# Attention blocks 8 to 14: who turns the probabilities, and when the next scores come

## What is computed

```python
def self_attn(x, Wq, Wk, Wv):
    Q, K, V = (x @ Wq, x @ Wk, x @ Wv)
    energy = jnp.einsum('bqd,bkd->bqk', Q, K)
    ...
    causal = (kidx[None, :] > kidx[:, None])[None]
    energy = jnp.where(pad | causal, NEG_INF, energy)
    score = jax.nn.softmax(energy / np.sqrt(DK), axis=-1)
    return jnp.einsum('bqk,bkd->bqd', score, V)
```

## Time and profile before

| | us |
|---|---|
| median of 3 runs | 1653.44 |
| lowest, highest | 1651.63, 1654.49 |
| profiled execution, whole | 1656.21 |
| its span, first to last instruction | 1654.4 |
| PE busy | 1617.4 |
| DVE busy | 862.5 |
| ACT busy | 572.2 |

### The profile page before, as it was taken

The page is one execution under the profiler, slowest core; times in us unless marked ns, Lnnn a source line. Parts: engine busy times, 40 slices in busy tenths (PEclk is TensorE's granted clock), DMA queues, the critical chain, the costliest instruction groups (busy, mean ns, idle before and its releaser), DMA issues. The chain is left out here.

```text
span 1654.4 us, 20692 instructions
## 1 busy us (share of the span) xinstructions
PE 1617.4 (98%) x7634; PEld 1334.5 (81%) x7634; DVE 862.5 (52%) x1760; ACT 572.2 (35%) x990; POOL 367.2 (22%) x562
## 2 busy tenths in 40 slices
PE   8999999999999999899999899999999999999999
PEld 6887888877788887678787687888888888888887
DVE  6757444477664435678888955342333232423311
ACT  5432121134221112466566533332323232323322
POOL 1212100022220100388888911000000000000000
PEclk9999999999999999799999999999999999999999
DMA  6302110131220104445545344121211112121100
GB/s 212 105 22 96 45 52 26 39 115 58 70 77 33 45 26 164 138 135 162 165 154 172 102 160 120 58 44 52 51 52 46 57 38 64 39 64 32 45 1 26
DMA packets 129930, 130.88 MB, mean 79 GB/s; under 512 B 70769, under 2 KB 70769, under 8 KB 129675
## 3 DMA queue, kind: packets, MB, share of 16 engines
q1 hardware_dynamic: 128032, 126.10, 24.5%
q10 hardware_dynamic: 1797, 3.46, 0.6%
HBM read 87.34 MB, written 42.18 MB: 78 GB/s over the span
## 5 line engine op out<-in xcount | busy, mean ns | idle before, releaser
L747 PE MATMUL banks<-split_q,split 128*128 128x512 f32 x2328 | 568.1, 393 | 4.6 <-POOL split L1563 3.2
L747 PE MATMUL banks<-split 128*128 128x512 f32 (+5 forms) x2304 | 543.1, 385 | 10.8 <-DVE split L1688 5.9
L747 PEld LDWEIGHTS banks<-split_q,split 128*128 128x128 f32 x2328 | 433.4, 188 | 96.9 <-POOL split L1563 4.1
L747 PEld LDWEIGHTS banks<-split 128*128 128x128 f32 (+3 forms) x2304 | 414.5, 185 | 107.0 <-issue 8.1
L747 PE MATMUL banks<-split,split_q 128*128 128x512 f32 (+3 forms) x1728 | 392.4, 379 | 6.8 <-DVE split_q L1688 4.1
L747 PEld LDWEIGHTS banks<-split,split_q 128*128 128x128 f32 x1728 | 308.7, 189 | 57.9 <-DVE split_q L1688 4.9
L2194 DVE TENSOR_TENSOR split<-plain,split 128x512 fp32r<-128x512 f32 x128 | 88.4, 691 | 385.6 <-ACT split L1464 385.6
L1458 ACT ACTIVATE plain<-banks,small 128x512 f32<-128x512 f32 x128 | 88.2, 689 | 400.1 <-PE banks L747 400.1
L1688 DVE TENSOR_TENSOR split<-banks,split 128x512 fp32r<-128x512 f32 (+5 forms) x232 | 146.3, 638 | 152.9 <-ACT split L1145 152.3
L1145 ACT ACTIVATE split<-banks 128x512 fp32r<-128x512 f32 (+5 forms) x232 | 124.4, 557 | 247.2 <-PE banks L957 191.1
L1497 POOL TENSOR_TENSOR small<-small 128x1 f32<-128x1 f32 x64 | 13.1, 205 | 475.7 <-DVE small L1724 475.5
(11 more groups left out here) (156 smaller groups left out, 1275.3 us busy)
## 6 DMA issues: line engine op xcount, KB each, us to landing
plain<-in_x SPq DMA_DIRECT2D x64, 256.0 KB, 2.7
xo_scratch<-plain SPq DMA_DIRECT2D x32, 256.0 KB, 2.3
x_scratch<-plain SPq DMA_DIRECT2D x32, 256.0 KB, 2.0
plain<-x_scratch SPq DMA_DIRECT2D x32, 256.0 KB, 3.0
tile_x<-xo_scratch SPq DMA_DIRECT2D x32, 256.0 KB, 3.1
xg_scratch<-tile_x SPq DMA_DIRECT2D x32, 256.0 KB, 2.1
out<-plain SPq DMA_DIRECT2D x32, 256.0 KB, 2.1
tile_x<-x_scratch SPq DMA_DIRECT2D x28, 256.0 KB, 4.6
```

The lines of the kernel that those rows point to most:

```text
L747: mm = nc.tensor.matmul(out, left(c, l), right(c, r), start=start and c == 0 and (l, r) == PASSES[0], stop=stop and c == chunks - 1 and (l ...
```

## The change

`turned(i)` marks blocks 8 to 14 of each batch. For these:

- PE issues no T. SP stores each chunk of the row buffer to `p_scratch` as soon as `p_ready` comes (`store_p`), and loads it back in four transfers for each chunk with the squares exchanged (`load_p`). All stores of a block come first, then all its loads. They stand at the end of SP's iteration i-2, behind the store of x1 for block i-2.
- A new letter I: DVE transposes within the squares, from the row buffer into the bank that T used. The high and low parts (still letter T, for ACT and DVE) follow as before.
- The list has another order: all of S(i+1) stands ahead of V(i) on PE. In blocks 8, 9, 10, 12, 13 and 14, I comes behind S(i+1, 1); V(i, 0) comes behind the last S, and on ACT the parts of chunk 2 stand behind X(i+1). In block 11 the projections Q(3, m) stand around the first parts, and V(11, 0) ahead of the scores.

```diff
+        if turned(i) and n1 > n0:
+            g = i // 4 + 1
+            order += [("Q", g, 0), end[0], ("Q", g, 1), end[1], ("I", i, 0), ("I", i, 1), ("Q", g, 2), ("T", i, 0),
+                      ("Q", g, 3), ("T", i, 1), ("V", i, 0), ("I", i, 2), ("S", i + 1, 0), ("T", i, 2)]
+            order += [("S", i + 1, c) for c in range(1, n1)]
+            order += [("X", i + 1, 0), ("V", i, 1), ("V", i, 2)]
+        elif turned(i):
+            order += [end[0], ("S", i + 1, 0), ("S", i + 1, 1), ("I", i, 0), ("I", i, 1), ("T", i, 0), ("I", i, 2),
+                      ("S", i + 1, 2), ("T", i, 1)]
+            order += [("I", i, 3)] if n0 > 3 else []
+            order.append(end[1])
+            order += [("S", i + 1, 3)] if n0 > 3 else []
+            order += [("X", i + 1, 0), ("V", i, 0), ("T", i, 2), ("V", i, 1)]
+            order += [("T", i, 3)] if n0 > 3 else []
+            order += [("V", i, c) for c in range(2, n0)]
...
-            if kind == "T":
+            if kind == ("I" if turned(i) else "T"):
                 order.append(("p", b, i, c))
...
+                def store_p(i, c):
+
+                    n, at, w = squares_in(b, i, c), c * 512, width_of(i, c)
+                    if n > 1:
+                        sp.wait_ge(p_in[c], (n - 1) * QB * 16)
+                    sp.dma_start(p_dram[c, 0:P * w].rearrange("(p n) -> p n", n=w), Srow[:, i % 2, at:at + w]).then_inc(p_out[c], 16)
+
+                def load_p(i, c):
+
+                    at, w = c * 512, width_of(i, c)
+                    sp.wait_ge(p_out[c], squares_in(b, i, c) * 16)
+                    squares_of = p_dram[c, 0:P * w].rearrange("(q s c i r) -> i s c q r", q=QB, s=32, i=QB, r=32)
+                    for n in range(QB):
+                        sp.dma_start(Srow[32 * n:32 * n + 32, i % 2, at:at + w].rearrange(
+                            "p (c q r) -> p c q r", q=QB, r=32), squares_of[n]).then_inc(p_in[c], 16)
...
+                    if turned(i + 2):
+                        sp.wait_ge(p_ready, b * NB + i + 2 + 1)
+                        for c in range(chunks_of(i + 2)):
+                            store_p(i + 2, c)
+                        for c in range(chunks_of(i + 2)):
+                            load_p(i + 2, c)
...
-                    elif kind == "T":
+                    elif kind == "T" and not turned(i):
                         n = TURNS["p", b, i, c]
                         if c == 0:
                             pe.wait_ge(p_ready, b * NB + i + 1)
+                        if c == 0 and turned(i - 1):
+                            pe.wait_ge(tp_full, n)
                         pe.wait_ge(tp_free, n + 1)
...
+                    elif kind == "I":
+                        n, at, w = TURNS["p", b, i, c], c * 512, width_of(i, c)
+                        dve.wait_ge(p_in[c], squares_in(b, i, c) * QB * 16)
+                        dve.wait_ge(tp_free, n + 1)
+                        nc.vector.transpose(PS[:, 2 + n % 2, 0:w], Srow[:, i % 2, at:at + w]).then_inc(tp_full, 1)
```

More of the change, by code:

```diff
@@ L89, with turned, squares_in @@
 T_BEFORE = [sum(chunks_of(j) for j in range(i)) for i in range(NB + 1)]
+def turned(i):
+    return 8 <= i < NB - 1
+def squares_in(b, i, c):
+    return sum(turned(j) and c < chunks_of(j) for j in range(NB)) * b + sum(
+        turned(j) and c < chunks_of(j) for j in range(i + 1))
 def attention_order(b):
@@ L109, in attention_order @@
         end = [(kind, i - 1, 0) for kind in "AB"]
-        if n1 > n0:
+        if turned(i) and n1 > n0:
[13 more added lines that the diff above has]
+            order += [("V", i, c) for c in range(2, n0)]
+        elif n1 > n0:
             g = i // 4 + 1
@@ L250, in build @@
         xg_dram = nc.dram_tensor("xg_scratch", (B * S, E), F32, kind="Internal").ap()
+        p_dram = nc.dram_tensor("p_scratch", (C, P * 512), F32, kind="Internal").ap()
         h_dram = nc.dram_tensor("h_scratch", (TILE, E), F32, kind="Internal").ap()
@@ L433, in build @@
         h_out, hb_in = sem("h_out"), sem("hb_in")
+        p_out, p_in = [sem(f"p_out_{c}") for c in range(C)], [sem(f"p_in_{c}") for c in range(C)]
         block = ctx.enter_context(nc.Block())
```

## The result

The changed kernel took **1675.1 us** (median; 1669.8 to 1678.9), the kernel before 1652.9 us beside it. The ratio is 1.0132, with a 95% interval of 1.0109 to 1.0154: 22 us slower, where the prediction had 9 us slower, 1662. The direction held and the time lies within the range of 1648 to 1678, but the loss is more than twice the one forecast.

A forecast was written before the change was run, and what follows sets the result against it. PE was taken to bound the kernel, busy 1617.4 of 1654.4 us. Waits of 29 us less 20 us of transposes gave +9 us on the median of 1653.4, so 1662, with a range of 1648 to 1678.

The forecast's parts named there:

- the gain: PE, blocks 8 to 14: 84 transposes a batch go, 0.12 us each, 10.1 us a batch, 20.2 us in all.
- the waits: PE ahead of values in blocks 8 to 14: turned probabilities come late, 14.5 us a batch, 29 for both.
- The walk for block 12: Queues of SP, DVE and ACT from S(12, 3): V(12, 2) can start at 24.2, PE waits 3.7 us, 3.9 beside POOL.
- The sum: Whole kernel: 29 us of waits less 20 of transposes, +9 us on the median, 1662.
- rival C: Attention: clock falls as well after long waits, 3 to 10 us more, 1666 to 1672; chance 0.16.
- Rival B: DVE's queue, blocks 12 to 14: loads issue at about 0.33 us, turn stays hidden, 1651 or 1645; chance 0.22.
- Rival D: SP's row of loads: slower than four, 0.75 an issue gives 1673, 0.9 gives 1693; chance 0.12.
- E: Whole change: the list could hold back another engine's work, so nothing moves; given no chance.

The follow-up runs named there:

- mended lists: Changed kernel with another list for blocks 8 to 10 and 12 to 14: B early, each chunk turned and taken apart as its load arrives; 1641.4 us, ratio 0.9925.
- six low parts: New order without the turn (PE still transposes), low part of T(i, 2) in blocks 12 to 14 computed six times instead of once; 1681.0 us, ratio 1.0164.
- Experiment 1: Changed kernel with 4 to 12 matmuls that nobody reads put into five PE waits, 34 a batch; 1668.6 us, 1.0088 times before.
- experiment 8: Changed kernel with each chunk loaded back by one plain load instead of four of squares, values wrong; 1655.6 us, ratio 1.0014.
- the change again: Second trace of the unaltered changed kernel; 1672.5 us.
- B early: Changed kernel with B(i-1) moved behind the mask of S(i+1, 0) in blocks 8 to 10 and 12 to 14; 1653.7 us, ratio 0.9999; traced again 1650.9 us.
- the turn alone: Changed kernel with the turn but the lists of before, each I(i, c) right ahead of its T(i, c); 1688.7 us, ratio 1.0212.
- 6: New order without the turn (PE still transposes), low part of T(i, 2) in blocks 12 to 14 computed three times; 1658.1 us, ratio 1.0034.

## Why the prediction was wrong

**Nearly right: the gain.** 0.12 us a transpose, 20.2 us in all. The mended lists show 17 of them as time.

**Right: the waits.** 14.5 us a batch were forecast; the brackets make 12.8 and 13.7, and with the 0.2 us for each 14.2 and 15.5. That the sum fits so well is in part luck, for the misses cancel: block 13 was to wait 2.5 us and waited 1.4 and 1.3, block 10 of the first batch 0.4 for 1.2, while block 14 waited 2.0 for 1.5. The walk for block 12 gave 3.7 to 3.9 us at V(12, 2), the trace has 4.11, and its links are all there (timeline of block 12; zero of the walk is 272.43, the start of V(11, 1)):

```profile
276.16 1.78 SPq L581 DMA_DIRECT2D p_scratch<-plain  x4
...
278.19 10.14 SPq L589 DMA_DIRECT2D plain<-p_scratch  x16
...
290.58 0.33 DVE L2049 STREAM_TRANSPOSE banks<-plain 128x128 f32<-128x128 f32 x1 [0.68 <-DMA plain<-p_scratch]
290.82 0.71 DVE L1781 SCALAR_TENSOR_TENSOR plain<-plain,small 128x512 f32<-128x512 f32 x1
291.57 0.75 DVE L1783 SCALAR_TENSOR_TENSOR plain<-plain,small 128x512 f32<-128x512 f32 x1
292.24 0.29 DVE L1994 CUSTOM_DVE_ANT_0 plain<-banks,plain 128x128 f32<-128x128 f32 x1
292.26 1.28 POOL L1579 TENSOR_TENSOR plain<-plain 128x512 f32<-128x512 f32 x1 [11.33 <-DMA plain<-in_x]
...
292.92 0.77 DVE L1994 CUSTOM_DVE_ANT_0 plain<-plain 128x128 f32<-128x128 f32 x1 [0.19 <-DVE plain L2004]
...
294.11 1.79 ACT L1325 ACTIVATE plain<-plain,small 128x1792 f32<-128x1792 f32 x1 [6.93 <-DVE small L2010]
...
296.50 0.89 DVE L1741 TENSOR_TENSOR split<-banks,split 128x512 fp32r<-128x512 f32 x2 [2.43 <-ACT split L1198]
```

Stores at 3.7 (276.16), loads 2.0 later, 16 issues in 10.14 us (0.63 each; 0.65 taken from the earlier trace rows), the wait of DVE for the last load at I(12, 3), B(11) behind it, the last mask, the exponential of 1.79, high part, low part. One link was new: the second half of the mask took 0.77 instead of 0.29 us beside POOL's shift, which B had met before.

**Wrong: the clock, the term that the sum left out.** The sum was waits less transposes, 29 - 20, and had nothing for the clock. The forecast put the clock into rival C with a chance of 0.16, "a wait of 3.9 us in block 12 is the longest", once to three times a batch, 3 to 10 us. The trace has a fall behind five of the six waits of 2.0 to 4.1 us, two in the first batch and three in the second, 9 us in all: the upper end of C. Its price and its count were within what C said; its place in the argument was the error. A forecast of 29 us of waits, with one of 3.9 and one of 2.5 us a batch in it, contained the condition for C, so C was no alternative to the forecast but a term of it: 9 + 9 = 18, 1671. By what the traces measured the terms are 26.5 of waits, 17 of gain and 9 of clock, which is 18 or 19 of the 20 us by which the profiled spans differ.

The reason given against it was that "the matmuls around the wait are dense". The kernel with six low parts refutes that: there they are as dense as in the kernel before, and the clock falls behind five of six waits. Experiment 1 shows it from the other side: with the waits filled the clock stays at 2.4 GHz, and the kernel is about 8 us faster.

**Rival B** (1645 to 1651) fell: the sync engine issued the loads at 0.63 us. **Rival D** (a row slower than four loads) had over 11 us for 16 loads as its sign. They took 10.14 to 11.05 us, and once 11.65 in the second trace of the same kernel, with landings at 2.5 us: mostly as forecast, at the edge of D in the slowest row. The issue price is what parted B from the forecast, and experiment 8 shows that it was the right question: without the long row the brackets are 8.6 us a batch, where B had 9, and the kernel is at 1655.6, though even then not faster. **E** fell: the page counts 168 matmuls fewer.

**Left open.** +19.5 in the attention of the profiled pair, +20.0 in the span and +22.2 in the medians; the last 2 us come from which executions were profiled, 3.3 us above the median before and 1.1 after. What stays open is what decides whether the clock falls behind a wait of 2.0 to 3.2 us: two executions of the same kernel differ.

## What to carry to other kernels

When work leaves TensorE and its product comes back later, sum up the waits first, and then charge the clock for waits as long as those here, 2 us and more, as a term of the sum, not as a rival: 1.6 us for each 3.4 at half clock; here a third of the waits on top (9 on 26.5), with six low parts half (9.6 on 17.9). A wait that can't be removed may be filled with matmuls nobody reads, but moving the step that the chain hangs on was worth more (21 us for one step of VectorE's list). Look for it behind the first wait in an in-order queue: what stood there, B(i-1), needed nothing of what the queue waited for.

## What the runs showed of the hardware

- **The clock behind short waits.** Of 28 waits of 2.0 to 4.5 us ahead of values in blocks 8 to 14, in six traces (the change and the change again, B early and again, the turn alone, six low parts), 23 had a stretch at 1.2 GHz that began between 1.8 us before and 1.4 behind the wait's end; five, of 2.05, 2.40, 2.91, 3.07 and 3.17 us, had none. Of the waits of 1.0 to 1.9 us in all these traces and in those of experiments 1, 6 and 8 none had. Every stretch was 3.4 or 6.8 us long, and one of 3.4 costs 1.6 us: twelve matmuls of 512 columns at 4.60 instead of 3.04 us. The Trainium skill, "TensorE: Matmul & The Clock Gate", section "HAM oscillation — how this bites in real kernels", reckons the penalty as half of the throttled time; the trace agrees, with 1.6 us for 3.4.
- **Issues of loads.** SP is held 0.63 to 0.73 us by each of 16 loads in a row that put squares of 128-byte pieces across (10.14 to 11.65 us for the 16), 0.55 by a plain load of the same row, 0.45 by each of four stores; from the first store's issue to the first load's 2.0 us pass.
- **VectorE's transpose within the squares**, from the row buffer into PSUM, takes 0.71 us for 128x512, the mean of 36 in the group's row, and 0.33 for 128x128.
